# Recurrent gates in another order and another packing, part of the attention exponentials done head by head, one stage of products shifted by a tile

## The chip, the cores and the metric

The program runs on one core of a Trainium2 chip. The metric is the device time in microseconds of one execution. The kernel before takes 8204.93 us in the median of three runs (8202.91 to 8206.75).

## The reference

Four batch rows of 1024 tokens with 256 features go through two blocks. What matters here is cut to this:

```python
def step(carry, x_t):                       # 1024 steps, one after another
    h0, c0, h1, c1, a = carry
    h0, c0 = lstm_cell(concat(x_t, a), h0, c0)      # g = x@Wi.T + bi + h@Wh.T + bh -> i, f, gg, o
    h1, c1 = lstm_cell(h0, h1, c1)                  # c2 = sig(f)*c + sig(i)*tanh(gg); h2 = sig(o)*tanh(c2)
    attn  = softmax(h1 @ Wq.T @ context.T)          # 64 context rows
    mixed = attn @ context
    a2 = tanh(concat(mixed, h1) @ Wo.T + bo)
    return (h0, c0, h1, c1, a2), a2
x = x + scan(step, layernorm(x))
x = x + ffn_quantized(layernorm(x))         # round, x @ W_in, exact gelu, round, @ W_out
x = x + attention_16_heads(layernorm(x), ctx)   # softmax(q k / 4 + mask) * group_prob @ v @ wo, 64 keys a head
x = x + mixture_of_8_experts(layernorm(x))
```

## The kernel before

The work is written by hand: each engine has its own instruction stream in program order, and semaphores tie them together. The stages follow one another: `front` (layernorm, folding of weights), `scan` (the 1024 recurrent steps), `add_attention_and_normalize`, `ffn_hidden`, `output_and_queries`, `attention`, `route` and the experts.

In `scan`, the state of a layer lies with its 256 features on the partitions, four batch columns for each half `k`. A product of state and weight takes the state as the stationary operand (4 columns, or 8 where the state is read together with four zero columns beside it) and streams 64 weight columns. The 256 units of a gate are cut into four blocks `j` that go to four column groups of the array, so four matmuls run side by side, on output partitions `32j` onward. `product` (L356) issues 8 matmuls for each gate (two halves `k`, four blocks `j`): 32 for the four gates. Gates i and g share one bank (`IG`): with the zero columns, i lands in rows 4 to 7 and g in rows 0 to 3 of each block. The third part of the bank, 64 columns wide, is added up over the recurrent, the input and the attention product, on top of the bias that ScalarE's `seed` (L426) wrote there.

When a bank is complete, VectorE transposes it in 32x32 blocks (`turn`, L492) so that units lie on partitions again, and ScalarE takes tanh of it. The sigmoids are made from tanh, with the halves folded into the weights. The cell's new value comes from one scan instruction over 24 columns (L581): three elements for each value, whose factors and addends were laid into the tile `scanned`. For one layer the order before is:

- ScalarE: tanh of f into `tanh_f` (L431), tanh of i and g into `scanned` (L433), tanh of o (L436), tanh of the cell (L438), a copy of the cell into `c` (L439), the next seed (L426).
- VectorE: turn f, turn i and g, `(tanh_f + 1) * c` into `scanned` (L577), turn o, the scan (L581), the new h (L583).
- TensorE: f, i, g, o of `wa` for layer 0 (L361 with `rec_wa`), then `wh1` for layer 1, then, when h of layer 0 is there, `wi1`, then `wh0` of f, i, g for the next step. When h of layer 1 is there: the scores (L372), `woh`, the o part of `wh0`, then `wx` of f and i, the spreading of the softmax total (L398: four matmuls of a single column), the mixing (L372), `wx` of g and o.

`ffn_hidden` works on 32 tiles of 128 tokens. TensorE turns tile t (L801) and then computes the products of tile t-5 (L811: 8 matmuls of 512 bf16 columns); ScalarE copies the turned tile (`split`, L825) and takes two gelus of tile t-5 (L832); VectorE makes the low part (L850), quantizes the next tile (L843, L846) and looks for the largest values (L858). The helper `in_steps` lays these out: a stage named with a lag works that many tiles behind. Inputs of four tiles share a buffer and there are two such buffers; `split` of a new group of four waits until all products of the group two back are done (`sum_done`).

`attention` has 32 tiles of 128 tokens, with 16 heads of 64 keys. For each tile VectorE adds the mask (L1177), takes the maximum per head (L1180), subtracts it (L1183), sums the exponentials (L1189), inverts (L1192) and adds the projected result (L1198). ScalarE fetches q (L1149), copies the turned weights (L1160, twice), takes all exponentials in one instruction over 1024 columns (L1153) and copies the mixed values (L1165). GpSimd multiplies by the group probability and by the inverted total (L1212, L1216) and adds a bias (L1209).

## Time and profile before

| | us |
|---|---|
| median of 3 runs | 8204.93 |
| profiled execution | 8210.56 |
| its span | 8208.8 |
| TensorE busy | 6973.1 (85%) |
| weight loads busy | 5941.0 (72%) |
| VectorE busy | 4544.6 (55%) |
| ScalarE busy | 3446.1 (42%) |
| GpSimd busy | 312.4 (4%) |

The mean granted TensorE clock is 0.984. A busy time counts the union of an engine's instructions, and idle time of an engine that others wait for shows only beside the rows of those others; so the shares tell little about a recurrence, and the order of the instructions within one step tells more.

### The profile page before, as it was taken

What the parts mean: (1) busy time and instruction counts of PE and PEld (TensorE: products, weight loads), DVE (VectorE), ACT (ScalarE), POOL (GpSimd) and SP (SyncE); (2) the same over time, 40 slices, a digit from 0 to 9 for tenths busy, and PEclk for the clock granted to TensorE, in tenths of its full rate; (3) what the DMA queues carried; (4) which work ended last, traced back from release to release, by engine and by line L of the source; (5) the groups of instructions that cost most, each with busy time, mean ns of one, the idle gap of its engine ahead of it and who ended that gap; (6) DMA issues with size and microseconds to landing.
All of it is one profiled execution on the core that took longest, in us unless ns stands there. A gap on an engine that the chain in (4) does not pass through costs nothing. (4 is left out here: it accounts for less than half of the span.)

```text
span 8208.8 us, 834179 instructions
## 1 busy us (share of the span) xinstructions
PE 6973.1 (85%) x388633; PEld 5941.0 (72%) x388641; DVE 4544.6 (55%) x21134; ACT 3446.1 (42%) x17105; POOL 312.4 (4%) x332
## 2 busy tenths in 40 slices
PE   7888888888888888888888888888888888868769
PEld 5777777777777777777777777777777777746546
DVE  5555555555555555555555555555555555566822
ACT  3444444444444444444444444444444444452422
POOL 0000000000000000000000000000000000002632
PEclk8999999999999999999999999999999999989889
DMA  3000000000000000000000000000000000000143
GB/s 113 5 0 0 5 0 0 0 0 5 0 0 0 5 0 0 0 0 5 0 0 0 5 0 0 0 5 0 0 0 0 5 0 0 0 14 11 62 148 109
DMA packets 94637, 101.99 MB, mean 12 GB/s; under 512 B 46570, under 2 KB 81904, under 8 KB 93424
## 3 DMA queue, kind: packets, MB, share of 16 engines
q1 hardware_dynamic: 89200, 88.73, 3.6%
q0 software_dynamic: 5376, 12.63, 0.4%
q14 instruction: 45, 0.37, 0.0%
q8 instruction: 16, 0.26, 0.0%
HBM read 79.75 MB, written 23.67 MB: 13 GB/s over the span
## 5 line engine op out<-in xcount | busy, mean ns | idle before, releaser
L361 PE MATMUL scan_sums<-rec_wh,scan_hT 128*4 128x64 f32 x131008 | 2394.5, 219 | 1.4 <-issue 1.3
L492 DVE STREAM_TRANSPOSE scan_sums<-scan_sums 128x64 f32<-128x64 f32 x6144 | 1551.8, 265 | 1129.8 <-PE scan_sums L361 1114.0
L361 PEld LDWEIGHTS scan_sums<-rec_wh,scan_hT 128*4 128x4 f32 x131008 | 1991.4, 89 | 2.2 <-issue 2.1
L361 PE MATMUL scan_sums<-rec_wa,scan_aT 128*4 128x64 f32 (+1 forms) x65536 | 1104.7, 219 | 474.6 <-ACT scan_aT L447 473.7
L361 PEld LDWEIGHTS scan_sums<-rec_wa,scan_aT 128*4 128x4 f32 (+1 forms) x65536 | 915.4, 88 | 663.7 <-ACT scan_aT L447 662.3
L361 PE MATMUL scan_sums<-rec_wx,scan_xT 128*4 128x64 f32 (+1 forms) x65536 | 1291.5, 219 | 3.4 <-issue 2.4
L361 PE MATMUL scan_sums<-rec_wi,scan_hT 128*4 128x64 f32 (+1 forms) x65536 | 1104.2, 219 | 145.0 <-issue 4.5
L361 PEld LDWEIGHTS scan_sums<-rec_wi,scan_hT 128*4 128x4 f32 (+1 forms) x65536 | 914.4, 88 | 334.5 <-DVE scan_hT L583 328.9
L361 PEld LDWEIGHTS scan_sums<-rec_wx,scan_xT 128*4 128x4 f32 (+1 forms) x65536 | 1023.9, 89 | 4.1 <-issue 2.9
L431 ACT ACTIVATE scan_tanh_f<-scan_sums 128x8 f32<-128x8 f32 x2048 | 364.1, 178 | 1185.9 <-DVE scan_sums L492 1185.8
L426 ACT ACTIVATE scan_sums<-rec_bias 128x192 f32<-128x192 f32 x2050 | 686.7, 335 | 303.9 <-PE scan_sums L408 6.1
L447 ACT ACTIVATE scan_aT<-scan_a_sum 128x8 f32<-128x8 f32 x1024 | 182.0, 178 | 1457.5 <-DVE scan_a_sum L598 1455.3
L372 PE MATMUL scan_scores<-rec_kp,scan_hT 128*4 128x64 f32 x16384 | 416.6, 219 | 372.6 <-DVE scan_hT L583 372.6
L372 PEld LDWEIGHTS scan_scores<-rec_kp,scan_hT 128*4 128x4 f32 x16384 | 227.6, 85 | 558.1 <-DVE scan_hT L583 558.1
L433 ACT ACTIVATE scan_scanned<-scan_sums 128x16 f32<-128x16 f32 x2048 | 393.0, 192 | 517.6 <-DVE scan_sums L492 502.1
L583 DVE SCALAR_TENSOR_TENSOR scan_hT<-scan_tanh_o,scan_sums 128x8 f32<-128x8 f32 x2048 | 335.9, 164 | 466.5 <-ACT scan_sums L438 466.0
L587 DVE TENSOR_REDUCE scan_neg_max<-scan_scores 128x1 f32<-128x65 f32 x1024 | 231.4, 226 | 517.4 <-PE scan_scores L372 517.4
L442 ACT ACTIVATE scan_exps<-scan_scores,scan_neg_max 128x64 f32<-128x64 f32 x1024 | 321.5, 314 | 430.9 <-DVE scan_neg_max L587 430.1
L581 DVE TENSOR_TENSOR_SCAN scan_sums<-scan_scanned 128x24 f32<-128x24 f32 x2048 | 443.6, 217 | 62.6 <-ACT scan_scanned L433 0.2
L372 PE MATMUL scan_a_sum<-rec_woh,scan_hT 128*4 128x64 f32 x16384 | 416.5, 219 | 0.0
L372 PE MATMUL scan_scores<-rec_vp,scan_expsT 128*4 128x64 f32 x16384 | 416.5, 219 | 0.0
L596 DVE SCALAR_TENSOR_TENSOR scan_a_natural<-scan_scores,scan_inv,scan_from_h 128x64 f32<-128x64 f32 x1024 | 290.8, 284 | 222.3 <-PE scan_scores L372 222.2
(265 smaller groups left out, 6480.6 us busy)
## 6 DMA issues: line engine op xcount, KB each, us to landing
experts_bias<-in_b SPq DMA_DIRECT2D x40, 640.0 KB, 4.3
moe_w<-in_w SPq DMA_DIRECT2D x16, 1024.0 KB, 14.7
slots_x<-scan_blank SPq DMA_DIRECT2D x40, 129.0 KB
experts_x<-slots_x SPq DMA_DIRECT2D x40, 129.0 KB
w_xres<-in_x_steps SPq DMA_DIRECT2D x8, 512.0 KB, 7.3
w_xres<-in_x SPq DMA_DIRECT2D x4, 1024.0 KB, 12.2
x_rows<-w_xres SPq DMA_DIRECT2D x4, 1024.0 KB, 8.5
a_rows<-scan_stage SPq DMA_DIRECT2D x224, 16.0 KB, 1.5
```

The lines of the kernel that those rows point to most:

```text
L361: last = nc.tensor.matmul(sums[layer][BANK[g]][32 * j:32 * j + ROWS[g], 0:64], state[:, k, FIRST[g]:FIRST[g] + ROWS[g]], weight[:, k, j, 6 ...
L372: last = nc.tensor.matmul(bank[32 * j:32 * j + B, 0:64], state[:, k, :], weight[:, k, j, :], start=k == 0, stop=k == 1, skip_group_check=True)
L426: nc.scalar.activation(layer_sums[l][:, :, 0:64], w["bias"][:, l, :, :], ACT.Copy).then_inc(seeded[l], 1)
L431: nc.scalar.activation(tanh_f[l][:], gates_of[l][F][:, :, 0:B], ACT.Tanh).then_inc(f_tanh[l], 1)
L433: nc.scalar.activation(ig_terms[l], gates_of[l][IG][:, :, 0:2 * B].rearrange("p k (f b) -> p k f b", f=2), ACT.Tanh).then_inc(c_terms[l], 1)
L442: nc.scalar.activation(exps[:], scores[:, 0:S], ACT.Exp, bias=neg_max[:], accum_out=total[:]).then_inc(exps_done, 1)
L447: nc.scalar.activation(state_of(aT), a_sumT.rearrange("p (k u) -> p k u", k=2)[:, :, 0:B], ACT.Tanh).then_inc(a_ready, 1)
L492: nc.vector.transpose(turned[l][g], sums[l][g][:, 0:64]).then_inc(gates_turned[l][g], 1)
L581: nc.vector.tensor_tensor_scan(cell[l], flat[l][:, 0], flat[l][:, 1], 0.0, ALU.mult, ALU.add).then_inc(c_done[l], 1)
L583: nc.vector.scalar_tensor_tensor(state_of(hT[l]), tanh_o[l][:], 1.0, tanh_c[l].rearrange("p (k b) -> p k b", k=2), ALU.add, ALU.mult).then ...
L587: nc.vector.tensor_reduce(neg_max[:], scores[:, 0:S + 1], AX.X, ALU.max, negate=True).then_inc(max_done, 1)
L596: nc.vector.scalar_tensor_tensor(a_natural[:], mixed, inv[:], from_h[:], ALU.mult, ALU.add).then_inc(a_scaled, 1)
```

## The change

Four things change.

1. `product` takes the gates in the order i, g, f, o where the caller names none. VectorE turns `IG` first and then f. ScalarE takes tanh of i and g first, into a tile `tanh_ig`, and then tanh of f, straight into `scanned` (`f_factor`). VectorE's small instruction now makes `(tanh_i + 1) * tanh_g` (`input_term`), and the copy of the cell goes into `scanned` too (`c_factor`).
2. Gate o is packed: its 64 units of a block are cut into two halves of 32. Each half is a product with 32 streamed columns and 8 stationary ones, the first half landing in rows 0 to 3, the second in rows 4 to 7, both in the same 32 columns. The turn of o covers 128x32 instead of 128x64.
3. In `attention`, the first 6 heads (`LONE`) are done by ScalarE one by one: an exponential of 64 columns with the negated maximum as its bias, read from the scores' PSUM bank, and with `accum_out` for its sum. VectorE subtracts and sums only for the other 10. On ScalarE the copy of the mixed values stands between the 6 single exponentials and the exponential of the 10. The scores of a tile now wait for the 6 exponentials of the tile two before.
4. In `ffn_hidden`, TensorE's products follow the turning by 4 tiles instead of 5.

```diff
-                def product(layer, state, weight, gates=(GATE_F, GATE_I, GATE_G, GATE_O), done=None):
+                def product(layer, state, weight, gates=(GATE_I, GATE_G, GATE_F, GATE_O), done=None):
...
+                        packed = g in HALVED
+                        for half in range(2 if packed else 1):
+                            first, rows = (B * (1 - half), 2 * B) if packed else (FIRST[g], ROWS[g])
+                            width = 32 if packed else 64
+                            for k in range(2):
+                                for j in range(4):
+                                    last = nc.tensor.matmul(sums[layer][BANK[g]][32 * j:32 * j + rows, 0:width],
+                                                            state[:, k, first:first + rows],
+                                                            weight[:, k, j, 64 * g + 32 * half:64 * g + 32 * half + width], start=False,
...
+                        act.wait_ge(gates_turned[l][IG], n)
+                        nc.scalar.activation(tanh_ig[l][:], gates_of[l][IG][:, :, 0:2 * B].rearrange("p k (f b) -> p f k b", f=2),
+                                             ACT.Tanh).then_inc(ig_tanh[l], 1)
                         act.wait_ge(gates_turned[l][F], n)
-                        nc.scalar.activation(tanh_f[l][:], gates_of[l][F][:, :, 0:B], ACT.Tanh).then_inc(f_tanh[l], 1)
-                        act.wait_ge(gates_turned[l][IG], n)
-                        nc.scalar.activation(ig_terms[l], gates_of[l][IG][:, :, 0:2 * B].rearrange("p k (f b) -> p k f b", f=2),
-                                             ACT.Tanh).then_inc(c_terms[l], 1)
+                        nc.scalar.activation(f_factor[l], gates_of[l][F][:, :, 0:B], ACT.Tanh).then_inc(c_terms[l], 1)
...
+                    width = 32 if g == O else 64
+                    nc.vector.transpose(turned[l][g][:, 0:width], sums[l][g][:, 0:width]).then_inc(gates_turned[l][g], 1)
...
-                in_steps(pe, [(turn, 0), (products, 5)], NB // 2, 2 * B)
+                in_steps(pe, [(turn, 0), (products, 4)], NB // 2, 2 * B)
...
-                    pe.wait_ge(shifted, number(g, b))
+                    pe.wait_ge(lone_done, LONE * number(g, b))
...
+                def lone_exps(g, b):
+                    act.wait_ge(shifted, number(g, b) + 2)
+                    for h in range(LONE):
+                        nc.scalar.activation(probs[b % 2][:, h, :], heads_of[b % 2][:, h, :], ACT.Exp, bias=neg_high[b % 2][:, h:h + 1],
+                                             accum_out=total[b % 2][:, h:h + 1]).then_inc(lone_done, 1)
...
-                in_steps(act, [(fetch, 0), (keep_turned, 3), (exps, 1), (keep_mixed, 3)])
+                in_steps(act, [(fetch, 0), (keep_turned, 3), (lone_exps, 1), (keep_mixed, 3), (exps, 1)])
...
-                    nc.vector.tensor_tensor(probs[s][:], heads_of[s], high[s][:].unsqueeze(2).broadcast_to([P, H, S]),
-                                            ALU.subtract).then_inc(shifted, 1)
+                    nc.vector.tensor_tensor(probs[s][:, LONE:H, :], heads_of[s][:, LONE:H, :],
+                                            neg_high[s][:, LONE:H].unsqueeze(2).broadcast_to([P, H - LONE, S]), ALU.add).then_inc(shifted, 1)
```

On TensorE, the loop body of the recurrence, from the attention product `rec_wa` up to the scores, reads before:

```order
L361 MATMUL scan_sums<-rec_wa,scan_aT 4x64 x8
L361 MATMUL scan_sums<-rec_wa,scan_aT 8x64 x16
L361 MATMUL scan_sums<-rec_wa,scan_aT 4x64 x8
L361 MATMUL scan_sums<-rec_wh,scan_hT 4x64 x8
L361 MATMUL scan_sums<-rec_wh,scan_hT 8x64 x16
L361 MATMUL scan_sums<-rec_wh,scan_hT 4x64 x8
```

and now:

```order
L367 MATMUL scan_sums<-rec_wa,scan_aT 8x64 x16
L367 MATMUL scan_sums<-rec_wa,scan_aT 4x64 x8
L367 MATMUL scan_sums<-rec_wa,scan_aT 8x32 x16
L367 MATMUL scan_sums<-rec_wh,scan_hT 8x64 x16
L367 MATMUL scan_sums<-rec_wh,scan_hT 4x64 x8
L367 MATMUL scan_sums<-rec_wh,scan_hT 8x32 x16
```

The 16 matmuls of i and g moved ahead of the 8 of f, and the 8 matmuls of o with 64 columns became 16 with 32 columns.

On VectorE, one layer of a step reads before:

```order
L492 STREAM_TRANSPOSE scan_sums<-scan_sums 128x64 x2
L577 SCALAR_TENSOR_TENSOR scan_scanned<-scan_tanh_f,scan_c 128x8
L492 STREAM_TRANSPOSE scan_sums<-scan_sums 128x64
L581 SCALAR_TENSOR_TENSOR scan_sums<-scan_scanned 128x24
L583 SCALAR_TENSOR_TENSOR scan_hT<-scan_tanh_o,scan_sums 128x2x4
```

and now:

```order
L499 STREAM_TRANSPOSE scan_sums<-scan_sums 128x64 x2
L584 SCALAR_TENSOR_TENSOR scan_scanned<-scan_tanh_ig 128x8
L499 STREAM_TRANSPOSE scan_sums<-scan_sums 128x32
L589 SCALAR_TENSOR_TENSOR scan_sums<-scan_scanned 128x24
L591 SCALAR_TENSOR_TENSOR scan_hT<-scan_tanh_o,scan_sums 128x2x4
```

The small instruction between the turns reads the tanh of i and g now, and the turn behind it is half as wide.

On ScalarE, one tile of the attention stage in its steady state reads before:

```order
L1149 ACTIVATE ffn_hidden<-ffn_hidden 128x256
L1160 ACTIVATE ffn_hidden<-attn_turned 128x512
L1160 ACTIVATE ffn_hidden<-attn_turned 128x512
L1153 ACTIVATE ffn_hidden<-ffn_hidden 128x1024
L1165 ACTIVATE ffn_hidden<-attn_mixed 128x256
```

and now:

```order
L1160 ACTIVATE ffn_hidden<-ffn_hidden 128x256
L1176 ACTIVATE ffn_hidden<-attn_turned 128x512
L1176 ACTIVATE ffn_hidden<-attn_turned 128x512
L1165 ACTIVATE ffn_hidden<-attn_scores,ffn_hidden 128x64 x6
L1181 ACTIVATE ffn_hidden<-attn_mixed 128x256
L1169 ACTIVATE ffn_hidden<-ffn_hidden 128x640
```

Six single-head exponentials stand where the one over 1024 columns stood, and the remaining one, over 640 columns, comes after the copy of the mixed values.

## Rows read from the trace of the kernel before

**Rows 1.** Stretches: window, length, busy PE, PEld, DVE, ACT, POOL, granted clock, DMA.

```profile
78.00:7254.00 7176.00, 6182.77 (x384520) 5404.82 (x384520) 3992.55 (x19700) 3075.05 (x16368) 20.64 (x56) 1.00 0.01 2
7277.00:7374.00 97.00, 71.04 (x313) 31.72 (x320) 72.42 (x166) 61.27 (x97) 0.00 (x0) 0.92 0.04 13
7556.00:7754.00 198.00, 153.87 (x1024) 87.18 (x1024) 172.24 (x191) 92.68 (x161) 145.38 (x96) 0.94 0.00 0
```

**Rows 2.** The instruction that closes a step: duration min/median/max, first and last start.

```profile
L447 ACT ACTIVATE scan_aT<-scan_a_sum x1024: 177/178/178, 77.9 to 7253.7; 128x8 f32<-128x8 f32 x171
```

**Rows 3.** Timeline of layer 0 in one step (start us, us, engine, line).

```profile
4008.86 1.08 PE L361 MATMUL scan_sums<-rec_wa,scan_aT 128*4 128x64 f32 x64 [0.46 <-ACT scan_aT L447]
...
4009.34 0.27 DVE L492 STREAM_TRANSPOSE scan_sums<-scan_sums 128x64 f32<-128x64 f32 x1 [0.21 <-PE scan_sums L361]
...
4009.76 1.08 PE L361 MATMUL scan_sums<-rec_wh,scan_hT 128*4 128x64 f32 x64
4009.78 0.27 DVE L492 STREAM_TRANSPOSE scan_sums<-scan_sums 128x64 f32<-128x64 f32 x1 [0.18 <-PE scan_sums L361]
4009.96 0.15 DVE L577 SCALAR_TENSOR_TENSOR scan_scanned<-scan_tanh_f,scan_c 128x8 f32<-128x8 f32 x1
4010.01 0.27 DVE L492 STREAM_TRANSPOSE scan_sums<-scan_sums 128x64 f32<-128x64 f32 x1
4010.08 0.19 ACT L433 ACTIVATE scan_scanned<-scan_sums 128x16 f32<-128x16 f32 x1 [0.27 <-DVE scan_sums L492]
...
4010.31 0.22 DVE L581 TENSOR_TENSOR_SCAN scan_sums<-scan_scanned 128x24 f32<-128x24 f32 x1
...
4010.97 1.08 PE L361 MATMUL scan_sums<-rec_wi,scan_hT 128*4 128x64 f32 x64
```

**Rows 4.** Timeline of TensorE later in the same step.

```profile
4013.74 0.63 PE L361 MATMUL scan_sums<-rec_wx,scan_xT 128*4 128x64 f32 x32
...
4014.36 0.21 PE L398 MATMUL scan_a_sum<-scan_total,w_ident 128*4 128x1 f32 x8
```

**Rows 5.** Groups by line: busy us, mean ns, idle before.

```profile
L433 ACT ACTIVATE scan_scanned<-scan_sums 128x16 f32<-128x16 f32 x2048 | 393.0, 192 | 517.6 <-DVE scan_sums L492 502.1
L431 ACT ACTIVATE scan_tanh_f<-scan_sums 128x8 f32<-128x8 f32 x2048 | 364.1, 178 | 1185.9 <-DVE scan_sums L492 1185.8
```

**Rows 6.** Groups by line: transposes of two widths.

```profile
L591 DVE STREAM_TRANSPOSE scan_expsT<-scan_exps 128x64 f32<-128x64 f32 x1024 | 250.9, 245 | 255.3 <-ACT scan_exps L442 255.3
L533 DVE STREAM_TRANSPOSE scan_stage<-scan_part 128x128 f32<-128x128 f32 x56 | 17.5, 312 | 9.6 <-POOL scan_part L327 9.6
```

**Rows 7.** Group by line: the matmuls with a single streamed column.

```profile
L398 PE MATMUL scan_a_sum<-scan_total,w_ident 128*4 128x1 f32 x8192 | 221.2, 166 | 1.8 <-issue 1.1 <-ACT scan_exps L442 0.7
```

**Rows 8.** Timeline of `ffn_hidden`: TensorE's turns of a group, ScalarE's copy behind it.

```profile
7313.08 0.44 PE L801 MATMUL hidden_turned<-w_ident,hidden_xq 128*128 128x128 f32 x2 [1.60 <-DVE hidden_xq L846]
...
7315.22 0.44 PE L801 MATMUL hidden_turned<-w_ident,hidden_xq 128*128 128x128 f32 x2
...
7322.43 0.39 ACT L825 ACTIVATE hidden_parts<-hidden_turned 128x256 bf16<-128x256 f32 x1 [1.37 <-PE hidden_summed L811]
...
7323.92 0.44 PE L801 MATMUL hidden_turned<-w_ident,hidden_xq 128*128 128x128 f32 x2 [1.61 <-DVE hidden_xq L846]
```

**Rows 9.** One line of `attention`: the mask addition, first and last start.

```profile
L1177 DVE TENSOR_TENSOR attn_scores<-attn_scores,ffn_hidden x32: 1207/1223/1233, 7560.8 to 7735.1; 128x1024 f32<-128x1024 f32 x32
```

**Rows 10.** Timeline of `attention`: one tile's subtraction and sum on VectorE.

```profile
7647.03 1.23 DVE L1183 TENSOR_TENSOR ffn_hidden<-attn_scores,ffn_hidden 128x1024 f32<-128x1024 f32 x1
...
7648.18 1.21 DVE L1189 TENSOR_REDUCE ffn_hidden<-ffn_hidden 128x16 f32<-128x1024 f32 x1
```

**Rows 11.** Groups by line: ScalarE's exponentials with and without a sum.

```profile
L442 ACT ACTIVATE scan_exps<-scan_scores,scan_neg_max 128x64 f32<-128x64 f32 x1024 | 321.5, 314 | 430.9 <-DVE scan_neg_max L587 430.1 <-issue 0.8
L442 ACT ACTIVATION_READ_ACCUMULATOR scan_exps<-scan_scores,scan_neg_max 128x1 f32 x1024 | 197.6, 193 | 0.0
L1153 ACT ACTIVATE ffn_hidden<-ffn_hidden 128x1024 f32<-128x1024 f32 x32 | 33.8, 1058 | 16.2 <-DVE ffn_hidden L1183 16.2
```

More of the change, by code:

```diff
@@ L355, in _ @@
             def _(pe):
-                def product(layer, state, weight, gates=(GATE_F, GATE_I, GATE_G, GATE_O), done=None):
+                def product(layer, state, weight, gates=(GATE_I, GATE_G, GATE_F, GATE_O), done=None):
                     for g in gates:
-                        for k in range(2):
-                            for j in range(4):
-                                last = nc.tensor.matmul(sums[layer][BANK[g]][32 * j:32 * j + ROWS[g], 0:64],
-                                                        state[:, k, FIRST[g]:FIRST[g] + ROWS[g]],
-                                                        weight[:, k, j, 64 * g:64 * g + 64], start=False,
-                                                        stop=done is not None and g != GATE_I and k == 1, skip_group_check=True)
+                        packed = g in HALVED
[7 more added lines that the diff above has]
+                                                            weight[:, k, j, 64 * g + 32 * half:64 * g + 32 * half + width], start=False,
+                                                            stop=done is not None and g != GATE_I and k == 1 and (half == 1 or not packed),
+                                                            skip_group_check=True)
                         if done is not None and g != GATE_I:
@@ L1084, in attention @@
         mixedT = [m.sbuf(f"mixedT{i}", [P, KC, P]) for i in range(2)]
[L1085 removed]
+        LONE = 6
+        neg_high, total, inv = (([m.sbuf(f"{n}{i}", [P, H]) for i in range(2)]) for n in ("neg_high", "total", "inv"))
         scores = [m.psum(f"scores{i}", (P, KC, 512)) for i in range(2)]
@@ L1669, in bias_rows @@
         rows = np.zeros((4, 32, GATES, 64), bias.dtype)
-        for g, first in enumerate((0, 0, B, 0)):
-            rows[:, first:first + B, g, :] = gate_blocks(bias)[g][:, None, :]
+        blocks = gate_blocks(bias)
+        for g, first in ((0, 0), (1, 0), (2, B)):
+            rows[:, first:first + B, g, :] = blocks[g][:, None, :]
+        for g in (3,):
+            for half in range(2):
+                rows[:, B * half:B * half + B, g, 0:32] = blocks[g][:, None, 32 * half:32 * half + 32]
         return rows.reshape(P, GATES, 64)
```

39 lines of the change are left out of this document (20 added, 19 removed).

## The prediction

> **What bounds the kernel now.** I read the stretches first, then the repetition of one step, then the timeline inside it. The recurrence takes 7176 of 8208.8 us and TensorE's granted clock is 1.00 there, its upper level of 2.4 GHz [rows 1]. The instruction that ends a step starts 1024 times between 77.9 and 7253.7, so a step costs 7175.8 / 1023 = 7.01 us [rows 2]. A nanosecond on the chain of one step is 1 us of the run, and the same nanosecond in each of the two layers is 2 us.
>
> Inside a step TensorE is mostly busy but does not set the pace [rows 3]. From the start of the attention product (4008.86), the f bank is ready for VectorE at 4009.34 and the bank of i and g at 4009.78, two gates later, so a gate costs 0.22. The turn of i and g takes 0.27; ScalarE starts its tanh at 4010.08, 0.03 behind; that takes 0.19 and the scan starts at 4010.31. The turn of o, started at 4010.01, ends at 4010.28, so it is no later than the tanh. After the scan the path runs through tanh of the cell and h to the next product at 4010.97; the change leaves these 0.66 us alone. Layer 1 repeats the pattern.
>
> **The recurrence, moved gates.** The last bank that the scan needs is still the third gate of the product: i and g before, f now. So f is ready at 4009.78, and i and g after two gates, 4009.34 + 0.22 = 4009.56. Their turn ends at 4009.83 and ScalarE's tanh runs from 4009.86 to 4010.05, beside the turn of f (4009.78 to 4010.05). VectorE is free for that turn: an instruction followed a turn 0.18 after its start (4009.78, 4009.96), and 4009.56 + 0.18 is before 4009.78 [rows 3]. ScalarE's tanh of f starts at 4010.08 as the tanh of i and g did, but covers 8 columns instead of 16: 178 ns instead of 192 [rows 5]. That is the whole gain on the chain, 14 ns a layer, if nothing takes its place: 0.014 x 2048 = 28.7 us. The copy of the cell only changes its target; it lies behind the tanh of the cell, hidden by the 0.2 us until h, and I cost it at nothing.
>
> What could take its place is VectorE. Its small instruction now waits for the tanh of i and g, 4010.05 + 0.03 = 4010.08 instead of 4009.96, and queued behind it are the turn of o and the scan. The turn of o starts 0.05 later (as 4009.96 to 4010.01), at 4010.13. Two transposes that differ by 64 columns differ by 312 - 245 = 67 ns [rows 6], so 32 columns fewer save 0.034; the turn then holds VectorE for 0.18 - 0.034 = 0.14, until 4010.27. The scan can start at 4010.26 + 0.03 = 4010.29 by the tanh of f. So the turn's end stays just in front, and the scan starts 0.014 earlier than before. If the narrower turn cost as much as the wide one, VectorE would be free at 4010.31: the gain is 0 and not negative. I take 28.7 us, with 0 and 29 as ends. Tanh of o starts later too, at 4010.40, but ScalarE only needs it done with the cell's tanh at 4010.54.
>
> **The recurrence, packed o.** A product shows 64 matmul records in 1.08 us, each 0.22 long, four side by side: (1.08 - 0.22) / 15 = 0.057 for each four [rows 3]. Gate o had 4 such fours, 0.23 us. Now it has 8 with half the columns. The lowest a four can cost is seen where one column is streamed: 8 records in 0.21 us, each 0.166 long, leave 0.044 for 7 starts, 0.025 a four [rows 4, 7]. So a narrow four costs between 0.025 and 0.057. The single-column row shows that the fixed part is small, and half of 0.057 is 0.029, so I take 0.03: o takes 0.24, as before within 0.02, and is ready at 4010.02, in front of the turn that now starts at 4010.13. There are five such products in a step; the others lie in gaps. Before `wi` TensorE has (4009.76 + 1.08 - 0.22 = 4010.62) to 4010.97 [rows 3], about 0.3 us of slack for two; before the spreading (4013.74 + 0.63 - 0.22 = 4014.15) to 4014.36, about 0.2 us for one [rows 3, 4]. Cost: nothing. It stays nothing up to 0.045 a four (7 x 0.016 = 0.11, what o may be late).
>
> A rule speaks against this part. The Trainium skill, "TensorEngine Tiling (Array Packing)", section Instruction Overhead, says that each matmul has about 60 cycles of overhead, a free dimension of 1 being as slow as one of 60, and advises against tiling a dimension that is already small. Read literally, 32 columns would cost as much as nearly 64, and the third rival below would hold. The single-column row only half agrees: 0.025 us is 60 cycles at 2.4 GHz, but the full four here costs 0.057.
>
> **`ffn_hidden`.** Four tiles take 7323.92 - 7313.08 = 10.84 us, 2.71 a tile, while two turns with nothing in between but products are 7315.22 - 7313.08 = 2.14 apart [rows 8]. The difference is waiting. ScalarE's copy of a tile stands behind the gelus of the products just done, and at each new group of four it waits 1.37 us more, since the last products of the group two back are issued only after the turn of the new group's first tile. With products 4 behind, they are issued one step earlier, and the gelus find theirs done. The inputs of the first product of a group are complete, since the low part of its fourth tile precedes the quantizing of the tile turned in that step. What is left is TensorE at 2.14 and VectorE at 72.42 / 32 = 2.26 [rows 1]. I take 2.25: (2.71 - 2.25) x 26 tiles after the slower start = 12, and 1 more for the shorter tail: 13 us. Ends: 8 (only the group waits go, 7 x 1.2) and 17.
>
> **`attention`.** Mask additions start 32 times from 7560.8 to 7735.1: 174.3 / 31 = 5.62 us a tile [rows 9]. VectorE is busy 172.24 / 32 = 5.38 of it, so it sets the pace, GpSimd 4.54 and ScalarE 2.90 [rows 1]. The subtraction and the sum, 1.23 and 1.21 [rows 10], lose 384 of 1024 columns each, at 67 / 64 = 1.05 ns a column: 0.40 each, and VectorE would allow 5.62 - 0.80 = 4.82. ScalarE gives up 1.06 and takes on an exponential over 640 columns (between 8 columns in 0.178 and 1024 in 1.058: 0.73) and 6 pairs of exponential and reading of the sum. A pair takes at least 0.31 and at most 0.314 + 0.193 = 0.51; the reading began 0.21 after the exponential in the recurrence, so 0.21 + 0.19 = 0.40 is the middle [rows 11]. ScalarE then has 2.90 - 1.06 + 0.73 + 6 x 0.40 = 4.97, less what overlaps. I take 4.95: 0.67 x 32 = 21, less 1 for the longer way of the last tile: 20 us. Ends: 26 (VectorE alone) and 0 (0.51 a pair: 5.63). The new wait of the scores has room: of the two periods between one use of a bank and the next, 9.9 us, the scores, the three VectorE instructions and the six exponentials need under 8.
>
> **Sum.** 28.7 + 13 + 20 = 62 us from the profiled execution's 8210.6: 8149. The median of the runs lies 5.7 us below that execution, so 8143. No measurement of this kernel tells less than about 0.2%, 16 us, from no change.
>
> **Rivals.**
> 1. VectorE takes the place of the tanh: the turn of o costs the same for half the columns, or a turn behind a turn is held longer. The scan stays at 4010.31. Against it: 67 ns for 64 columns; for it: the margin is 0.02 us. Time 8143 + 29 = 8172. Chance 0.17.
> 2. ScalarE becomes the bound of `attention` at 5.6 us a tile: no gain there. For it: no row shows six such pairs in a stream; against it: neighbours on ScalarE overlap elsewhere. 8163. Chance 0.09.
> 3. The slower side: a four with 32 columns costs what one with 64 does, 0.057. Then o is ready 0.20 later, at 4010.21; turned until 4010.35, so the scan is 0.04 late in each layer; and in front of `wi` TensorE has 0.46 more to do in a slack of about 0.3, 0.14 late instead of 0.04 in layer 0. Together 0.18 a step, 184 us, instead of a gain of 29: 8143 + 29 + 184 = 8356. It decides from 0.045 a four on. Against it stands the single-column row, for it only that the eight fours of a packed gate, with 8 stationary columns, appear nowhere. Chance 0.10.
>
> **How the numbers follow.** The forecast, all three gains, has 0.64. Its own range is 8130 to 8160, from the ends of the three terms. The range of 8 in 10 takes in the first two rivals together: 8125 to 8188. Faster by over 0.2% are the forecast and rivals 1 and 2 but for a small part: 0.86. Within 0.2%: 0.04, where a small loss in the recurrence meets the gains of the two stages. Slower: 0.10.
>
> **What would show it.** Right: the closing tanh starts every 6.98 us instead of 7.01; the scan starts when the tanh of f ends; product records of 32 columns come at 0.03 a four; tiles of `ffn_hidden` every 2.2 to 2.3 us without the wait of 1.37; mask additions every 4.8 to 5.1 us. Wrong: the scan starting at the end of the turn of o while the tanh is long done; a wait of VectorE on TensorE in front of that turn; `wi` starting with no idle time in front; ScalarE without idle time in `attention`.

## The result and the profile after

The changed kernel takes 8158.83 us in the median of five runs (8158.43 to 8160.45), the kernel before beside it 8204.93 (8202.25 to 8207.31). The ratio is 0.9944, with a 95% interval of 0.993 to 0.9957: 46 us faster. One execution of the kernel with the new `attention` alone (below) took 9765.67 us at a granted clock of 0.626 and is left out of its numbers. One slip in the text ahead of the prediction: in the bank of i and g it is i that lands in rows 0 to 3 and g in rows 4 to 7; no number rests on it.

The page of the changed kernel gives the busy times of the engines:

```profile
PE 7204.2 (88%) x470544; PEld 6373.2 (78%) x470545; DVE 4419.2 (54%) x21132; ACT 3380.3 (41%) x17489; POOL 313.6 (4%) x332
```

TensorE is busier than before (7204.2 against 6973.1 us), since the packed gate has twice the matmuls, and the time is shorter all the same. (The profile shows two records for each matmul of these products: the 32 matmuls of a product before are x64, and the counts in profile lines are of records.) The three stretches that answer to [rows 1], cut at the first and last instruction of each stage (columns as there):

```profile
80.00:7244.00 7164.00, 6420.89 (x466368) 5838.76 (x466368) 3894.37 (x19700) 2974.14 (x16368) 20.53 (x56) 1.00 0.01 2
7267.50:7350.20 82.70, 72.45 (x320) 32.05 (x320) 70.13 (x165) 56.99 (x97) 0.00 (x0) 0.90 0.04 15
7531.70:7704.30 172.60, 146.89 (x1024) 86.47 (x1024) 146.65 (x191) 131.72 (x543) 144.70 (x95) 0.95 0.00 0
```

Cut in the same way, the stages before took 96.4 (`ffn_hidden`) and 197.0 us (`attention`); they gave 13.7 and 24.4. The span fell from 8208.8 to 8158.7, by 50.1, which leaves 12 for everything else. The recurrence gave that. The instruction that closes a step, for [rows 2]:

```profile
L454 ACT ACTIVATE scan_aT<-scan_a_sum x1024: 177/178/178, 80.0 to 7243.8; 128x8 f32<-128x8 f32 x171
```

1023 steps take 7163.8 instead of 7175.8 us: 12.0 less, 7.003 us a step instead of 7.014. But the first step is done 2.1 us later than before (80.0 against 77.9). Both differences have some play. Two kernels of the experiments have the recurrence of the kernel before, and their traces give 7173.0 and 7172.9 us, with the first step done at 77.6 and 79.4; two further ones with that of the changed kernel give 7164.2 and 7163.9. So the recurrence gave between 9 and 12 us. Inside a step the timeline of layer 0, weight loads left out, for [rows 3]:

```profile
4003.78 0.18 ACT L454 ACTIVATE scan_aT<-scan_a_sum 128x8 f32<-128x8 f32 x1 [1.42 <-DVE scan_a_sum L606]
...
4004.01 1.13 PE L367 MATMUL scan_sums<-rec_wa,scan_aT 128*8 128x64 f32 x80 [0.42 <-ACT scan_aT L454]
4004.71 0.49 DVE L499 STREAM_TRANSPOSE scan_sums<-scan_sums 128x64 f32<-128x64 f32 x2 [0.44 <-PE scan_sums L367]
4004.96 1.12 PE L367 MATMUL scan_sums<-rec_wh,scan_hT 128*8 128x64 f32 x80
4005.01 0.18 ACT L438 ACTIVATE scan_tanh_ig<-scan_sums 128x16 f32<-128x16 f32 x1 [0.85 <-DVE scan_sums L499]
4005.22 0.17 DVE L584 SCALAR_TENSOR_TENSOR scan_scanned<-scan_tanh_ig 128x8 f32<-128x8 f32 x1
4005.23 0.18 ACT L441 ACTIVATE scan_scanned<-scan_sums 128x8 f32<-128x8 f32 x1
4005.31 0.23 DVE L499 STREAM_TRANSPOSE scan_sums<-scan_sums 128x32 f32<-128x32 f32 x1
4005.45 0.22 DVE L589 TENSOR_TENSOR_SCAN scan_sums<-scan_scanned 128x24 f32<-128x24 f32 x1
...
4005.89 0.16 DVE L591 SCALAR_TENSOR_TENSOR scan_hT<-scan_tanh_o,scan_sums 128x8 f32<-128x8 f32 x1 [0.23 <-ACT scan_sums L445]
4006.11 1.13 PE L367 MATMUL scan_sums<-rec_wi,scan_hT 128*8 128x64 f32 x80
```

Read three things in it. The order is the one that was forecast: tanh of i and g, the small instruction and the tanh of f side by side, the turn of o, the scan. From one product to the next (4004.01 to 4004.96) TensorE takes 0.95 us where it took 0.90 (4008.86 to 4009.76 in [rows 3]): the packed o costs 0.05 more, 0.27 instead of 0.22. And the scan starts when the tanh of f is done (4005.23 + 0.18, and 0.03 behind it), though the turn of o is still shown as running until 4005.54.

One step can't show nanoseconds, so I worked out over all steps of both traces the median start of each instruction from the start of the closing tanh. In layer 0, in ns:

```
                              before   after
bank of the third gate turned   1151    1155
tanh that the scan waits for    1449    1454   lasting 193, now 181
scan                            1674    1668
h                               2119    2113
```

Layer 0 gives 6 ns. Behind layer 1, h is 11 earlier (4213 instead of 4224), and a step is 12 shorter by its mean. Groups by line, for [rows 5] and [rows 6] (busy us, mean ns of one | idle before):

```profile
L441 ACT ACTIVATE scan_scanned<-scan_sums 128x8 f32<-128x8 f32 x2048 | 372.6, 182 | 81.2 <-DVE scan_sums L499 1.4
...
L499 DVE STREAM_TRANSPOSE scan_sums<-scan_sums 128x64 f32<-128x64 f32 x4096 | 1000.4, 265 | 1224.6 <-PE scan_sums L367 1224.5
L499 DVE STREAM_TRANSPOSE scan_sums<-scan_sums 128x32 f32<-128x32 f32 x2048 | 461.0, 225 | 2.0 <-PE scan_sums L367 1.9
```

The tanh of f takes 182 ns here, 178 in [rows 5]. The narrow turn saves 40 ns of 265, close to the 34 of the prediction.

In `ffn_hidden` TensorE's turns, for [rows 8], with ScalarE's copy behind one:

```profile
7313.41 0.44 PE L809 MATMUL hidden_turned<-w_ident,hidden_xq 128*128 128x128 f32 x2
...
7315.56 0.44 PE L809 MATMUL hidden_turned<-w_ident,hidden_xq 128*128 128x128 f32 x2
7316.03 0.38 ACT L833 ACTIVATE hidden_parts<-hidden_turned 128x256 bf16<-128x256 f32 x1 [0.42 <-PE hidden_turned L809]
...
7321.99 0.44 PE L809 MATMUL hidden_turned<-w_ident,hidden_xq 128*128 128x128 f32 x2
```

Four tiles take 7321.99 - 7313.41 = 8.58 us, 2.14 each instead of 2.71. No copy waits for a product any more, TensorE runs without a pause and sets the pace.

In `attention` the mask addition, for [rows 9]:

```profile
L1193 DVE TENSOR_TENSOR attn_scores<-attn_scores,ffn_hidden x32: 1222/1223/1233, 7535.5 to 7686.8; 128x1024 f32<-128x1024 f32 x32
```

(7686.8 - 7535.5) / 31 = 4.88 us a tile, where it was 5.62. The timeline of a tile:

```profile
7613.84 1.22 DVE L1193 TENSOR_TENSOR attn_scores<-attn_scores,ffn_hidden 128x1024 f32<-128x1024 f32 x1
...
7615.10 1.23 DVE L1196 TENSOR_REDUCE ffn_hidden<-attn_scores 128x16 f32<-128x1024 f32 x1
...
7616.43 0.83 DVE L1199 TENSOR_TENSOR ffn_hidden<-attn_scores,ffn_hidden 128x640 f32<-128x640 f32 x1
...
7617.17 0.81 DVE L1205 TENSOR_REDUCE ffn_hidden<-ffn_hidden 128x10 f32<-128x640 f32 x1
7617.31 0.32 ACT L1165 ACTIVATE ffn_hidden<-attn_scores,ffn_hidden 128x64 f32<-128x64 f32 x1
7617.51 0.21 ACT L1165 ACTIVATION_READ_ACCUMULATOR ffn_hidden<-attn_scores,ffn_hidden 128x1 f32 x1
7617.60 0.33 ACT L1165 ACTIVATE ffn_hidden<-attn_scores,ffn_hidden 128x64 f32<-128x64 f32 x1
...
7618.70 1.22 DVE L1193 TENSOR_TENSOR attn_scores<-attn_scores,ffn_hidden 128x1024 f32<-128x1024 f32 x1
7619.10 0.39 ACT L1181 ACTIVATE ffn_hidden<-attn_mixed 128x256 f32<-128x256 f32 x1
...
7619.53 0.48 PE L1148 MATMUL attn_y<-ffn_wo,ffn_hidden 128*128 128x256 f32 x1 [0.51 <-ACT ffn_hidden L1181]
```

Subtraction and sum went from 1.23 and 1.21 [rows 10] to 0.83 and 0.81. VectorE has no wait in the tile and sets the pace. ScalarE's pairs follow each other 0.29 apart (7617.31, 7617.60), and its busy time is 131.72 / 32 = 4.12 us a tile.

### The profile page after: what moved, and what is told of

The parts are those of the page before. It is cut to its first block and busy times, and to the rows that moved or that the text cites. A ratio compares the mean times of both kernels' runs of the same rounds, so it can differ in the third digit from the quotient of the medians.

```text
span 8158.7 us, 998374 instructions
## 1 busy us (share of the span) xinstructions
PE 7204.2 (88%) x470544; PEld 6373.2 (78%) x470545; DVE 4419.2 (54%) x21132; ACT 3380.3 (41%) x17489; POOL 313.6 (4%) x332
## 5 line engine op out<-in xcount | busy, mean ns | idle before, releaser
L367 PE MATMUL scan_sums<-rec_wh,scan_hT 128*8 128x64 f32 (+1 forms) x163760 | 2521.0, 209 | 0.1
L367 PEld LDWEIGHTS scan_sums<-rec_wh,scan_hT 128*8 128x8 f32 x163760 | 2130.2, 89 | 0.4 <-issue 0.2
L499 DVE STREAM_TRANSPOSE scan_sums<-scan_sums 128x64 f32<-128x64 f32 (+1 forms) x6144 | 1461.4, 252 | 1226.6 <-PE scan_sums L367 1226.4
L367 PE MATMUL scan_sums<-rec_wa,scan_aT 128*8 128x64 f32 (+2 forms) x81920 | 1158.4, 209 | 425.8 <-ACT scan_aT L454 425.5
L367 PEld LDWEIGHTS scan_sums<-rec_wa,scan_aT 128*8 128x8 f32 (+1 forms) x81920 | 1025.3, 89 | 557.1 <-ACT scan_aT L454 556.5
L367 PE MATMUL scan_sums<-rec_wx,scan_xT 128*8 128x64 f32 (+2 forms) x81920 | 1369.0, 209 | 2.9 <-issue 2.0
L367 PE MATMUL scan_sums<-rec_wi,scan_hT 128*8 128x64 f32 (+2 forms) x81920 | 1157.4, 209 | 35.0 <-issue 6.5
L367 PEld LDWEIGHTS scan_sums<-rec_wi,scan_hT 128*8 128x8 f32 (+1 forms) x81920 | 1025.4, 89 | 166.7 <-DVE scan_hT L591 159.9
L367 PEld LDWEIGHTS scan_sums<-rec_wx,scan_xT 128*8 128x8 f32 (+1 forms) x81920 | 1107.4, 89 | 3.8 <-issue 2.7
L438 ACT ACTIVATE scan_tanh_ig<-scan_sums 128x16 f32<-128x16 f32 x2048 | 378.0, 185 | 1620.2 <-DVE scan_sums L499 1618.8
```

What stands on the lines that cost most here:

```text
L367: last = nc.tensor.matmul(sums[layer][BANK[g]][32 * j:32 * j + rows, 0:width], state[:, k, first:first + rows], weight[:, k, j, 64 * g + 3 ...
L438: nc.scalar.activation(tanh_ig[l][:], gates_of[l][IG][:, :, 0:2 * B].rearrange("p k (f b) -> p f k b", f=2), ACT.Tanh).then_inc(ig_tanh[l], 1)
L499: nc.vector.transpose(turned[l][g][:, 0:width], sums[l][g][:, 0:width]).then_inc(gates_turned[l][g], 1)
```

## The experiments

### Each part alone

Four kernels take one part each; the other three parts are as before. In `ffn_hidden`:

```diff
-                in_steps(pe, [(turn, 0), (products, 5)], NB // 2, 2 * B)
+                in_steps(pe, [(turn, 0), (products, 4)], NB // 2, 2 * B)
```

> The kernel before with the products of ffn_hidden 4 tiles behind the turning, nothing else. Theory: the four parts of the change add up and this one is worth the stage's shortening seen in the profile after, 96.4 to 82.7 us, so 8205 - 14 = 8191. Rival: part of the shortening came from the other parts (a different clock phase at the stage's start), then it is under 8 us here: above 8197.

Measured: 8191.08 us (8189.14 to 8196.37) beside 8205.19, ratio 0.9983 (0.9974 to 0.9993): 14.1 us less, as in the whole change (13.7). The second kernel has the `attention` function of the changed kernel.

```diff
-                in_steps(act, [(fetch, 0), (keep_turned, 3), (exps, 1), (keep_mixed, 3)])
+                in_steps(act, [(fetch, 0), (keep_turned, 3), (lone_exps, 1), (keep_mixed, 3), (exps, 1)])
```

> The kernel before with the attention stage of the change alone. Theory: the stage goes from 197 to 173 us as after, so 8205 - 24 = 8181, and mask additions start every 4.87 us. Rival: ScalarE or GpSimd gave way only together with the other parts; then the stage is above 180 us.

Measured: 8181.83 us (8178.72 to 8187.26), ratio 0.9972 (0.9961 to 0.9982): 23.4 less. One line shows that this stage is as in the whole change, 4.88 us a tile:

```profile
L1185 DVE TENSOR_TENSOR attn_scores<-attn_scores,ffn_hidden x32: 1222/1223/1233, 7558.5 to 7709.8; 128x1024 f32<-128x1024 f32 x32
```

The third has only the new order of the gates; o is unpacked and turned 128x64.

```diff
-                def product(layer, state, weight, gates=(GATE_F, GATE_I, GATE_G, GATE_O), done=None):
+                def product(layer, state, weight, gates=(GATE_I, GATE_G, GATE_F, GATE_O), done=None):
...
+        HALVED = ()
```

> The kernel before with the gates in the order i, g, f, o alone; o stays 64 columns wide, 8 matmuls, turned at 128x64. Theory (VectorE's queue sets the scan's start: small instruction, 0.084 later the turn of o, which holds VectorE 0.173 when wide): the scan starts 0.032 later than before in each layer, 0.064 a step, so 8205 + 65 = 8270. Rival (only the tanh of f sets it, the turn's width does not matter): the recurrence gains 10 to 14 us as after, 8193.

Measured: 8197.15 us (8189.63 to 8200.76), ratio 0.999 (0.9981 to 1.0): 8.0 less and not 65 more. The interval touches 1, but each of the ten executions lies below each of the thirty of the kernel before (8202.92 at least). The lateness that I feared from the wide turn did not come. VectorE in layer 0 of this kernel:

```profile
4005.43 0.17 DVE L584 SCALAR_TENSOR_TENSOR scan_scanned<-scan_tanh_ig 128x8 f32<-128x8 f32 x1
4005.51 0.26 DVE L499 STREAM_TRANSPOSE scan_sums<-scan_sums 128x64 f32<-128x64 f32 x1
4005.68 0.18 DVE L589 TENSOR_TENSOR_SCAN scan_sums<-scan_scanned 128x24 f32<-128x24 f32 x1
```

The scan starts 0.25 behind the small instruction, where it was 0.23 (4005.22 to 4005.45) in the changed kernel; but it is recorded with 0.18 and there with 0.22, so it ends 0.43 behind in the one and 0.45 in the other. The start of a record is no measure of when the result is there. In medians over all steps the scan ends 1882 ns after the closing tanh, in the changed kernel 1885, before 1891.

The fourth packs o and keeps the order f, i, g, o.

```diff
+        HALVED = (GATE_O,)
...
+                    width = 32 if g == O else 64
```

> The kernel before with o packed in 32 columns alone; gates in the old order f, i, g, o. Theory: the tanh of i and g alone sets the scan's start there, the narrower turn and the later readiness of o are both hidden, so 8205 within 4 us and a step of 7.00. Rival: the packed product itself costs (TensorE reaches the product with wi late, or o is ready too late): over 8215.

Measured: 8215.74 us (8212.66 to 8218.14), ratio 1.0012 (1.0003 to 1.0022): 10.6 more. Its step-closing tanh runs from 81.0 to 7262.2, so 1023 steps take 7181.2, 5.4 more than before, and the first step is 3.1 later. Packing by itself costs time; the rival that expected a loss was right, the size being small.

Alone the parts give -14.1 - 23.4 - 8.0 + 10.6 = -34.9; together they give -46. `ffn_hidden` and `attention` give nearly the same alone and together, so most of the 11 between them lies in the recurrence; the end of the next part comes back to it.

### What the packing does in company

Packing undone in the changed kernel (o with 64 columns and 4 stationary ones, turned 128x64):

```diff
-        HALVED = (GATE_O,)
+        HALVED = ()
...
-                    width = 32 if g == O else 64
+                    width = 64
```

> The kernel after with the packing of o undone (64 columns, 8 matmuls, turn of 128x64), all else as after. Theory (the packing gains nothing, since the tanh of f holds the scan and a scan directly behind a wide turn ends no later): 8160 within 4. Rival (the packing is worth something in company, or its heavier feed of TensorE costs as it does alone, 10 us): 8149 by the cost, 8170 or more by the worth.

Measured: 8151.66 us (8150.65 to 8153.12), ratio 0.9936 (0.9919 to 0.9952). This is the best version found, 7 us under the changed kernel (6 by the kernels before that ran beside each); no run of the one reaches a run of the other. Of the times expected, 8149 came nearest, by which the packing costs in company what it costs alone. The closing tanh of a step, and the mask addition:

```profile
L454 ACT ACTIVATE scan_aT<-scan_a_sum x1024: 177/178/178, 77.6 to 7239.4; 128x8 f32<-128x8 f32 x171
...
L1193 DVE TENSOR_TENSOR attn_scores<-attn_scores,ffn_hidden x32: 1222/1223/1233, 7530.6 to 7681.9; 128x1024 f32<-128x1024 f32 x32
```

Against the changed kernel the first step is done 2.4 earlier and 1023 steps take 2.0 less (7161.8), which makes 4.4 of the 4.9 by which `attention` starts earlier; the stage itself is equal. So the packing costs about 2 in all steps but the first, which a second pair of traces bears out (7164.2 and 7162.1, both with eight heads). The 2.4 of the first step are hardly more than the 1.8 by which it differs between traces of one and the same recurrence (77.6 to 79.4). Another 2.5 of the two spans (8158.7 and 8151.3) lies behind `attention`, where the code is the same.

Only the turn made wide, with the product packed:

```diff
-                    width = 32 if g == O else 64
+                    width = 64
```

> The kernel after with o still in 32 columns on TensorE but turned at 128x64 by VectorE. Theory A: the scan starts about 0.03 later but takes 0.03 less, since it stands directly behind the turn; no change, 8155 to 8160. Theory of the prediction (a later start is a later end): 0.03 a layer, 8159 + 60 = 8219.

Measured: 8158.05 us (8156.52 to 8158.2), no change. The group of the scans says why:

```profile
L589 DVE TENSOR_TENSOR_SCAN scan_sums<-scan_scanned 128x24 f32<-128x24 f32 x2048 | 382.6, 187 | 0.0
```

It is recorded with 187 ns, with 217 in the changed kernel; in medians it starts at 1699 instead of 1668 and ends within 2 ns of it. The width of the turn is worth nothing.

Now f packed as o is:

```diff
-        HALVED = (GATE_O,)
+        HALVED = (GATE_F, GATE_O)
...
-                    width = 32 if g == O else 64
+                    width = 32 if g != IG else 64
```

> The kernel after with f packed like o (16 matmuls of 32 columns, turn of 128x32). The turn of f ends 0.04 earlier and so does its tanh. Theory A (in the kernel after the scan waits for the tanh of f; an instruction that waits at an idle VectorE takes 0.217, one that follows directly behind another 0.186): the scan of layer 0 still starts 1.67 after the closing tanh but takes 0.186, so the gate path gains 0.03 a layer. Theory B (VectorE's queue alone sets the scan's end): nothing gained on that path. In both, TensorE's feed of instructions may fall behind with 32 more records before wi: if it sustains one record in 0.0125, wi is about 0.2 late in layer 0 and the step is about 7.15, 8159 + 170 = 8330; if narrow fours keep their 0.029 pace, 8159 - 60 = 8099 by A, 8159 by B.

Measured: 8235.25 us (8234.75 to 8241.63), ratio 1.0038: 76 more than the changed kernel, and neither theory. TensorE and VectorE in layer 0:

```profile
4003.94 0.18 ACT L454 ACTIVATE scan_aT<-scan_a_sum 128x8 f32<-128x8 f32 x1 [1.42 <-DVE scan_a_sum L606]
...
4004.17 1.20 PE L367 MATMUL scan_sums<-rec_wa,scan_aT 128*8 128x64 f32 x96 [0.42 <-ACT scan_aT L454]
...
4005.19 1.17 PE L367 MATMUL scan_sums<-rec_wh,scan_hT 128*8 128x64 f32 x96
...
4005.64 0.22 DVE L589 TENSOR_TENSOR_SCAN scan_sums<-scan_scanned 128x24 f32<-128x24 f32 x1
```

From product to product it is 1.02 instead of 0.95, so a second packed gate costs 0.07 more. It comes ahead of f's bank: f is turned at 1224 ns instead of 1155. The turn is 0.034 shorter (231 ns), which leaves 0.034 for the tanh of f, and the scan starts at 1.70 (4003.94 to 4005.64) instead of 1.67. Layer 1 repeats it: in medians over all steps h of layer 0 is 34 ns later than in the changed kernel and h of layer 1 69, and the 1023 steps take 71.6 us more. With 3.9 in the first step that is the whole difference.

The second part of the expectation, a late `wi`, did not come. TensorE's idle time in front of `wi` went from 145 us in all (before) to 35.0 (changed kernel) to 7.3, but `wi` still starts 0.055 us after the record of h of layer 0 ends, as in the kernel before and in the changed one (0.054 in both). So no instruction in front of `wi` was on the chain.

The same with gate i of `wh1` ahead of the wait for the attention state, so that TensorE does 8 of the matmuls (16 records) while it would be idle:

```diff
+                    pe.wait_ge(seeded[1], n)
+                    product(1, hT[1], w["wh1"], (GATE_I,))
                     pe.wait_ge(a_ready, n)
                     product(0, aT, w["wa"], done=gates_summed[0])
-                    pe.wait_ge(seeded[1], n)
-                    product(1, hT[1], w["wh1"])
+                    product(1, hT[1], w["wh1"], (GATE_G, GATE_F, GATE_O))
```

> The run before (f packed too) with wh1 of gate i moved in front of the wait for the attention output, into TensorE's idle 0.4 us there. It takes 0.22 us out of the stretch in front of wi. If TensorE's feed is what makes wi late with f packed, most of the lateness goes: by theory A 8100 to 8140; if wi was not late there, no difference to the run before.

Measured: 8268.71 us (8266.95 to 8271.96), ratio 1.0077: worse than without the move by another 33, where I expected 8100 to 8140. The waits of TensorE (us in total, times, longest), its timeline, and the branch of its loop:

```profile
PE scan_sums L367 <- issue: 247.3, 1029, 3.7
```

```profile
4000.17 0.41 PE L367 MATMUL scan_sums<-rec_wh,scan_hT 128*8 128x64 f32 x16 [0.22 <-issue]
4000.40 1.20 PE L367 MATMUL scan_sums<-rec_wa,scan_aT 128*8 128x64 f32 x96
```

```profile
L420 PEldq COMPARE_BRANCH x1023: 76/208/220, 86.7 to 7342.4; - x171
```

The moved matmuls stand in a step with a wait of 0.22 that no semaphore explains, about once a step (1029 times). It is the place where TensorE's loop closes: `with pe.Fori(0, T - 1) as t: step(t)` (L420) has one step as its body, and each of its branches takes TensorE's sequencer 208 ns (76 the last time, when the loop is left). In medians the branch runs from 324 to 116 ns ahead of the closing tanh, a register operation follows until 23 ahead, and the first moved matmul starts 34 behind. In the changed kernel the same branch lies inside the 0.42 us in which TensorE waits for the closing tanh, and costs nothing. So half of the idle time that the move was to use is taken by the branch. The moved product then ends too late: the attention product starts 255 ns behind the closing tanh instead of 230, the tanh of i and g 22 later, and a step takes 32 ns more, which is the 33 us. That the move gained nothing elsewhere agrees with a `wi` that was not late before: it has 0.17 us of idle time in front now and starts 0.055 behind h again. A kernel with two steps in the body of TensorE's loop would test this reading; there is none.

Where a packed gate spends its time shows in the starts of its records, in medians over all steps. In the attention product of the changed kernel, fours of 64 columns start 0.056 apart. The fours of the packed o start 0.029 apart six times, as I took, then 0.054 and 0.046: 0.27 for the gate. With f and o packed, the first six of the sixteen are 0.029 apart, three about 0.05, and from there on they come every 0.033, with the weight loads evenly 0.0083 apart. That the instructions are handed out no faster than this, and that a lead gained over wide fours is used up by the narrow ones, is what fits; no run changes the supply alone. One more row speaks for it: the loop's branch starts 0.31 us before the last matmul of a step ends where nothing is packed, and 0.14 where o is. A rule of the Trainium skill stood against the packing ("TensorEngine Tiling (Array Packing)", section Instruction Overhead: a matmul of one column is as slow as one of 60, so a dimension that is small already should not be cut). The runs agree with its advice, and only in part with its size: packing makes a gate 1.2 times as long (0.27 to 0.22), where by that rule it would be nearly twice.

Does VectorE hold the scan? The small instruction reads a constant and waits for nothing, so the turn of o can start early. This kernel leaves out the input term of the cell (the product of the tanh of i and g), and everything else is computed:

```diff
-                        dve.wait_ge(ig_tanh[l], n)
-                        nc.vector.scalar_tensor_tensor(input_term[l], tanh_ig[l][:, 0].rearrange("p k b -> p (k b)"), 1.0,
+                        nc.vector.scalar_tensor_tensor(input_term[l], fixed[:, 0].rearrange("p k b -> p (k b)"), 1.0,
```

> The kernel after, with the small instruction between the turns reading a constant tile instead of the tanh of i and g, so that it no longer waits for ScalarE (the input term is left out of the computation). VectorE is then free for the scan from about 1.56 after the closing tanh. Theory A (the tanh of f holds the scan): nothing changes, 8159 within 4. Theory B (the small instruction and the turn of o behind it hold the scan): the scan ends earlier by up to 0.03 in each layer, 8100 to 8150.

Measured: 8158.94 us (8156.81 to 8159.85), no change. In medians the turn of o starts at 1447 ns instead of 1533, 86 earlier, and the scan at 1669 instead of 1668. What holds the scan is the tanh of f; the kernel with f packed agrees, where that tanh and the scan are both 34 ns late.

What stays open is 11 us between the parts alone and together. Order alone gives 8.0 by the medians; in company, with the packing undone, it gives 8204.01 - 8151.66 - 14.1 - 23.4 = 15, and the packing costs 10.6 in the old order but 6 to 7 in the new one. The profiled execution of the order alone (8189.63) was its fastest, and there 1023 steps run from 77.5 to 7235.0, 18.3 less than before. Two kernels with the same loop (this one and the unpacked one) differ by 4.3 us in it, in their profiled executions. Differences of this size in the recurrence are not explained by anything that I changed.

### The attention stage

Eight heads on ScalarE instead of six:

```diff
-LONE = 6
+LONE = 8
```

> The kernel after with 8 heads on ScalarE instead of 6. Theory (VectorE sets the pace of attention, ScalarE's pair of exponential and reading takes 0.29): VectorE loses 2 x 128 columns, 0.27 a tile, until GpSimd's 4.54 busy is in the way: 4.65 a tile instead of 4.87, 8159 - 7 = 8152. Rival (ScalarE's order is already what limits): no gain, or mask additions further apart than 4.87.

Measured: 8176.08 us (8172.7 to 8178.35), 17 more than the changed kernel, where I expected 7 less. Tiles are 5.38 us apart (7534.4 to 7701.2 over 31). In one of them:

```profile
7598.73 1.23 DVE L1193 TENSOR_TENSOR attn_scores<-attn_scores,ffn_hidden 128x1024 f32<-128x1024 f32 x1 [0.77 <-PE attn_scores L1118]
...
7599.73 0.44 ACT L1181 ACTIVATE ffn_hidden<-attn_mixed 128x256 f32<-128x256 f32 x1
...
7600.23 1.13 PE L1148 MATMUL attn_y<-ffn_wo,ffn_hidden 128*128 128x256 f32 x4 [1.09 <-ACT ffn_hidden L1181]
...
7601.19 1.04 PE L1129 MATMUL attn_turned<-w_ident,ffn_hidden 128*128 128x128 f32 x8
...
7602.07 1.88 PE L1118 MATMUL attn_scores<-ffn_hidden 128*128 128x512 f32 x4
...
7602.80 0.32 ACT L1165 ACTIVATE ffn_hidden<-attn_scores,ffn_hidden 128x64 f32<-128x64 f32 x1
...
7604.10 1.23 DVE L1193 TENSOR_TENSOR attn_scores<-attn_scores,ffn_hidden 128x1024 f32<-128x1024 f32 x1 [0.68 <-PE attn_scores L1118]
```

VectorE now waits 0.7 for the scores. Follow the releasers back: the scores stand behind the turning and the projection in TensorE's order, the projection waits 1.09 for ScalarE's copy of the mixed values, and that copy stands behind the eight exponentials, which wait for VectorE's maximum and subtraction. This is a loop over three engines, and no engine in it is full: from 7536 to 7700 (164 us) VectorE is busy 132.0, ScalarE 135.2 and TensorE 127.3.

Packing undone and eight heads:

```diff
-        HALVED = (GATE_O,)
+        HALVED = ()
...
-LONE = 6
+LONE = 8
```

> Both edits: packing of o undone and 8 heads on ScalarE. If they add up: 8153 within 4.

Measured: 8166.48 us (8164.09 to 8174.5), 10 less than with eight heads alone. The 8153 that I expected took over the gain of eight heads that did not come; by the measured parts (8151.66 + 17) it is 8169, so the two edits act nearly apart, and six heads stay the better number of the two.

The copy of the mixed values put back behind the exponential of the ten heads, as in the order before:

```diff
-                in_steps(act, [(fetch, 0), (keep_turned, 3), (lone_exps, 1), (keep_mixed, 3), (exps, 1)])
+                in_steps(act, [(fetch, 0), (keep_turned, 3), (lone_exps, 1), (exps, 1), (keep_mixed, 3)])
```

> The kernel after with the copy of the mixed values behind the exponential of the 10 heads, not between. Theory: ScalarE has over half a microsecond idle in each tile and the projection that reads the copy is a tile ahead of its use on VectorE, so nothing changes, 8159 within 3. Rival (the place was needed): the projection starts 0.6 later and the stage gets longer by up to 0.3 a tile, 8169.

Measured: 8176.7 us (8175.65 to 8181.15), 18 more, where I expected no change. The same loop closes, as ScalarE's order and TensorE's wait show:

```profile
7604.03 0.78 ACT L1169 ACTIVATE ffn_hidden<-ffn_hidden 128x640 f32<-128x640 f32 x1
7604.66 0.43 ACT L1181 ACTIVATE ffn_hidden<-attn_mixed 128x256 f32<-128x256 f32 x1
...
7605.14 0.70 PE L1148 MATMUL attn_y<-ffn_wo,ffn_hidden 128*128 128x256 f32 x2 [1.11 <-ACT ffn_hidden L1181]
```

The copy comes 0.6 later behind the larger exponential, and a tile takes 5.37 (7534.8 to 7701.2 over 31). So the place of the copy was worth 18 of the stage's 24 us.

## Why the prediction came out as it did

The forecast was 8143 and 62 us of gain; the median is 8158.8 and the gain 46. The direction held, the time lies inside the range, and of the three terms one was too large. In profiled executions the three gave 50.1, so 8160.5. From there I took off the 5.7 us by which the kernel before lies lower in its median; the changed kernel lies only 1.6 lower. That is another 4 us of the miss of 16, and the two stages gave 5 more than forecast against it.

- **The recurrence, moved gates (28.7 forecast, 9 to 12 measured with the packing in it).** The mechanism held: the scan waits for a tanh of 8 columns in place of one of 16, and nothing else took its place. The kernel in which the turn of o starts 86 ns earlier moves nothing. The term was mis-sized: 14 ns a layer, of which 4 to 6 came. The third bank is ready 4 ns later than by my "still the third gate", the tanh starts 1 ns later still, and the tanh of f takes 181 where I took 178 from another target. The 4 ns arise at the start of the product: its second four now starts 60 ns behind the first instead of 56, and all later ones keep their distance; that the weight loads of 8 columns, which now come first, are the reason is argued, not shown. The longer tanh goes with its new target, the tile for the scan: the copy of the cell, moved into the same tile, went from 172 to 176, the tanh of i and g, moved out of it, from 193 to 185, and the tanh of o, which keeps its tile, still takes 178. The step that failed is taking 14 ns as exact out of rows with other operands and targets, when each of these differences is 3 to 5 ns.
- **The turn of o.** I had it end 0.02 in front of the scan and priced rivals by it. The scan starts before that turn's record ends, and at equal ends its recorded length is 187 or 217 ns. So the margin that I worked out from starts was not the real one, and rival 1 fell as a mechanism. Its number, 8172, was 13 off where mine was 16 off; the forecast was not the closer one.
- **The packed product (nothing forecast, 2 to 11 measured).** A gate takes 0.27 and not 0.24. The cover that I named holds in a step: o's bank is still ready ahead of its turn, and `wi` has 0.03 us of idle time left of 0.14. But the packing bought nothing either: the narrow turn, its only gain, is worth nothing, and undoing it saves 7 us. Rival 3 did not come: narrow fours cost 0.029 at first and 0.033 when many follow each other, under the 0.045 from which it decides. Where a packed gate does stand on the chain, as f does, it costs 72 us of the recurrence: its bank is 0.07 late in each layer and the narrow turn gives back half.
- **`ffn_hidden` (13 forecast, 13.7 measured; 14.1 alone).** Right by its own steps. A tile takes 2.14 rather than 2.25: VectorE's busy time over the whole stretch, divided by its 32 tiles, gave 2.26, more than it needs for a tile in the steady part.
- **`attention` (20 forecast, 24.4 measured; 23.4 alone).** VectorE sets the pace at 4.88, near the 4.82 that I had for it alone. A pair on ScalarE takes 0.29 where I took 0.40, so ScalarE has room and rival 2 fell. My working missed the copy of the mixed values: I said that the scores have room by the use of their bank, and did not follow what stands ahead of them in TensorE's order. With the copy where it stood before, that step would have cost 18 us.

## What to carry to other kernels

Before an instruction is lengthened or moved on one engine, follow its in-order neighbours on the engine that waits for it, not only its own buffers: the loop through copy, projection, scores and mask addition cost 18 us with no engine busy all the time. A gain of a few nanoseconds on a repeated chain, worked out from rows with other operands and targets, came here at under half. Halving the columns of many small matmuls doubles the instructions; what that costs is set by whether the chain waits for that gate's bank (f: 72 us; o: 2 to 8 us of the recurrence). And before work is moved into an engine's idle time at the edge of a loop body, see what the sequencer does there: half of that idle time was the loop's own branch.

## What the hardware showed

- A VectorE scan that waits for a semaphore on an engine about to be free is recorded with 217 ns, the same scan directly behind a longer turn with 184 to 187, and both end at the same time. So the starts of records don't add up to ends where instructions follow closely. The Trainium skill, "Perfetto Trace Analysis", section DVE / Act Engine Instruction, says that a record runs from the start of execution to the acknowledged write, and that the next instruction may begin to fetch its operands once execution is over. The traces agree in that a record starts up to 0.1 us before the one ahead of it ends.
- TensorE's matmuls of 32 columns on four column groups start 0.029 us apart a four for the first six, and every 0.033 once sixteen fours follow each other, where fours of 64 columns start 0.056 apart.
- A taken branch of TensorE's loop occupies its sequencer for 208 ns, the last one, not taken, 76. While TensorE waited 0.42 us for ScalarE anyway it cost nothing; a product moved into that wait stood behind it, with 0.22 us of idle time in every step.
- An exponential of 64 columns with the reading of its sum takes ScalarE 0.29 us in a stream, though the two are recorded with 332 and 224 ns.
